# Query projection of a cross-attention kernel: seven block products of one Strassen level in place of eight

## What is computed

```python
# latents: 8 batches x 112 rows, 1024 wide; Wq: 1024 x 4096 (32 heads of 128)
q = (latents @ Wq).reshape(b, q_len, N_KV_HEADS, N_GROUPS, HEAD_DIM)
k = (hidden_states @ Wk).reshape(b, kv_len, N_KV_HEADS, HEAD_DIM)
v = (hidden_states @ Wv).reshape(b, kv_len, N_KV_HEADS, HEAD_DIM)
scores = jnp.einsum('bqhgd,bkhd->bhgqk', q, k) * scale
attn = jax.nn.softmax(scores.astype(jnp.float32), axis=-1).astype(q.dtype)
out = jnp.einsum('bhgqk,bkhd->bqhgd', attn, v)
```

## Time and profile before

| | us |
|---|---|
| median of 3 runs | 1857.2 |
| the runs | 1855.57, 1857.20, 1857.59 |
| the profiled execution | 1857.21 |
| its span, first to last instruction | 1855.3 |
| PE busy in the span | 1824.4 (98%) |
| ACT, DVE, POOL busy | 599.2, 636.9, 588.8 |

### The profile page before, as it was taken

How to read it: one execution, slowest core, us unless ns; L and a number is a source line. 1 busy time by engine, 2 the same in 40 slices (tenths; PEclk the granted TensorE clock), 3 DMA queues, 4 the chain that set the end, 5 groups by cost and what they waited for, 6 DMA issues and landing times.

```text
span 1855.3 us, 26708 instructions
## 1 busy us (share of the span) xinstructions
PE 1824.4 (98%) x9446; PEld 1645.2 (89%) x9446; DVE 636.9 (34%) x1114; ACT 599.2 (32%) x1156; POOL 588.8 (32%) x392
## 2 busy tenths in 40 slices
PE   8999999999999999999999999999999999999996
PEld 7989989799999988989998999899888988998886
DVE  3611122111111137713761475157344422212216
ACT  3221212122222246713761475157422213202321
POOL 2121200022222236533452255235455322222242
PEclk9999999999999999999999999999999999999998
DMA  8444412343654534422441244134244221111134
GB/s 276 156 163 153 148 68 108 93 140 124 207 187 134 176 127 156 142 79 68 151 151 61 86 162 127 51 113 139 100 144 163 80 97 51 57 57 53 49 102 170
DMA packets 108974, 225.78 MB, mean 122 GB/s; under 512 B 14976, under 2 KB 73344, under 8 KB 108032
## 3 DMA queue, kind: packets, MB, share of 16 engines
q1 hardware_dynamic: 108928, 225.14, 36.1%
...
## 4 chain that ended last, share of the span: by engine, by line
PE 68%; issue 21%; POOL 8%; DVE 1%; ACT 1%; DMA 0%; POOLq 0%; SPq 0%; ACTq 0%; DVEq 0%
PE bank L1133 22%; PE bank L1134 22%; PE bank L1135 22%; POOL tile_region L608 6%; POOL slab_split L577 2%; PE bank L1294 1%; PE bank L1166 0%; ACT slab_split L649 0%; PE bank L1195 0%; DVE small L863 0%; DMA mid_region<-k_latents_scratch 0%; DVE mid_region L856 0%; DMA slab_raw<-in_wkv 0%; POOLq L607 0%; DVE tile_region L1109 0%
## 5 line engine op out<-in xcount | busy, mean ns | idle before, releaser
L577 POOL TENSOR_TENSOR slab_split<-slab_raw,slab_split 128x1024 fp32r<-128x1024 f32 x126 | 301.9, 2397 | 783.8 <-ACT slab_split L649 783.8
L1133 PE MATMUL bank<-act_region,slab_split 128*128 128x448 f32 (+2 forms) x1376 | 501.0, 364 | 1.7 <-DVE mid_region L856 1.3
L1135 PE MATMUL bank<-act_region,slab_split 128*128 128x448 f32 (+2 forms) x1376 | 501.0, 364 | 0.0
L1134 PE MATMUL bank<-act_region,slab_split 128*128 128x448 f32 (+2 forms) x1376 | 500.7, 364 | 0.0
L608 POOL TENSOR_TENSOR tile_region<-tile_region,small 128x487 f32<-128x487 f32 x224 | 215.9, 1001 | 219.7 <-DVE small L939 219.7
L1133 PEld LDWEIGHTS bank<-act_region,slab_split 128*128 128x128 f32 x1376 | 258.4, 188 | 28.9 <-issue 2.3
L1134 PEld LDWEIGHTS bank<-act_region,slab_split 128*128 128x128 f32 x1376 | 258.4, 188 | 25.6
L1135 PEld LDWEIGHTS bank<-act_region,slab_split 128*128 128x128 f32 x1376 | 258.3, 188 | 24.8
L649 ACT ACTIVATE slab_split<-slab_raw 128x1024 fp32r<-128x1024 f32 x126 | 133.0, 1057 | 389.4 <-PE bank L1135 378.6
L1133 PE MATMUL bank<-mid_region 128*128 128x488 f32 (+2 forms) x480 | 199.0, 415 | 3.0 <-DMA mid_region<-k_latents_scratch 2.5
L976 DVE TENSOR_TENSOR y_region<-y_region,bank 128x512 f32 (+2 forms) x96 | 59.5, 620 | 365.7 <-PE bank L1135 365.7
...
## 6 DMA issues: line engine op xcount, KB each, us to landing
slab_raw<-in_slabs SPq DMA_DIRECT2D x126, 512.0 KB, 3.5
q_scratch<-y_region SPq DMA_DIRECT2D x16, 1792.0 KB, 7.6
...
```

The costliest lines, as they stand in the source:

```text
L577: pool.tensor_tensor(WS[s][1], RAWS[s], f32(WS[s][0]), ALU.subtract).then_inc(s_wlo, 1)
L1133: pe.matmul(out_ap, w[0], a[0], start=first, stop=False)
L1134: pe.matmul(out_ap, w[0], a[1], start=False, stop=False)
L1135: return pe.matmul(out_ap, w[1], a[0], start=False, stop=last)
```

## The change

A pair of heads is now one block product. The weights of the pair are a 2x2 of blocks (two heads, two halves of the contraction), the latents another (two halves of the contraction, two halves of the rows). Plain multiplication takes 8 block products of 4 k each; one level of Strassen's scheme (in Winograd's form) takes 7, of sums of blocks, and adds the results up.

- Four sums of latent blocks' halves (T1 to T4) are made once: nine steps and four splits on DVE (`row_sums`), four hi parts on ACT, 1792 columns each, between the `kl` and `vl` units. The `vl` units now take batches 4 to 7 first.
- For each pair POOL makes four sums of weight blocks from the two raw slabs, then the lo parts of seven blocks; ACT makes the seven hi parts (`block_hi`). Each block is 128x512. The seven split blocks WB and the raw slabs have one buffer each.
- For each pair PE runs seven products of 4 k x 3 = 12 matmuls of 448 columns. ACT copies the first product to SBUF; DVE makes seven sums (`combine`) that end in four half results C22, P1C, C21 and C12, in this order; ACT and DVE split these into QST.
- SP loads both slabs of a pair together and stores the pair's queries as before. The score tiles of the first step stand behind products 4, 5 and 6 of the last pair. Loads of the first two attention steps move, and the buffers of queries, keys and values in RB lie elsewhere.

```diff
+BLOCKS = ("A11", "S2", "S3", "S1", "A12", "A22", "S4")
+N_Q = len(BLOCKS)
+N_COMB = 7
+LAST_QUAD = {3: (0, 1, 2), 4: (3, 4), 5: (5, 6)}
...
         RAWS = [part(RAW, s * SLAB, SLAB) for s in range(2)]
...
+        def x_block(h, kh):
+            return [XT[h][:, l, 4 * kh:4 * kh + 4, :] for l in range(2)]
+
+        B11, B21, B12, B22 = x_block(0, 0), x_block(0, 1), x_block(1, 0), x_block(1, 1)
+        T2, T3, T4 = [t_block(RB, i * 2 * T_WORDS) for i in range(3)]
+        T1 = B12
+        TRAW = [part(YR, i * T_WORDS, T_WORDS).rearrange("p (k n) -> p k n", k=4) for i in range(2)]
...
+        WB = [[part(RC, (2 * i + l) * 512, 512) for l in range(2)] for i in range(4)]
+        WB += [[part(RD, (2 * i + l) * 512, 512) for l in range(2)] for i in range(2)]
+        WB += [[part(RA, l * XT_AT + 2 * NK * HALF, 512) for l in range(2)]]
+        SRAW = [part(FB, i * 512, 512) for i in range(4)]
+        WSRC = [RAWS[0][:, 0:512], SRAW[1], SRAW[2], SRAW[0], RAWS[0][:, 512:1024], RAWS[1][:, 512:1024], SRAW[3]]
+        W21 = RAWS[1][:, 0:512]
+        P1C, U3, C22, C21 = [part(FB, at, HALF) for at in (2048, 2496, 2944, 3500)]
+        U2, C12 = [part(YR, 8 * ROWS + i * HALF, HALF) for i in range(2)]
...
+            def load_pair(j):
+                for s in range(2):
+                    sp.dma_start(RAWS[s], slabs[T_Q + 2 * j + s]).then_inc(s_rawq, 16)
+
+            load_pair(0)
...
+                    if n == N_UNITS - 1:
+                        sp.wait_ge(s_blo, N_Q - 1)
+                        load_pair(1)
...
-            def store_pair(kv, g, c, slot):
-                sp.wait_ge(s_ev, c + 1)
+            def store_pair(j):
+                kv, g, slot = j // 4, 2 * (j % 4), j % 2
+                sp.wait_ge(s_qlo, FREE + 4 * (j + 1))
                 sp.dma_start(q_d[kv, :, :, :, g * SQ:(g + 2) * SQ].rearrange("p b l c -> p (b l) c"),
                              part(YR, slot * 4 * ROWS, 4 * ROWS).rearrange("p (b c) -> p b c", b=2 * B)
                              ).then_inc(s_qst[slot], 16)
...
-            q_heads(0)
...
-            with sp.Fori(2, NKV) as kv:
-                q_heads(kv)
+            store_pair(0)
+            for j in range(1, PAIRS):
+                if j < PAIRS - 1:
+                    sp.wait_ge(s_blo, N_Q * j + N_Q - 1)
+                    load_pair(j + 1)
+                else:
+                    sp.wait_ge(s_blo, N_Q * PAIRS)
+                    for s in range(2):
+                        sp.dma_start(RAWS[s], slabs[T_WO + s]).then_inc(s_raw[s], 16)
+                    sp.wait_ge(s_q, N_Q * j + 3)
+                    load_qk(0, 1, 1, 1)
+                    load_v(0, 1, 1, 1)
+                store_pair(j)
+                if j == 8:
...
+                    load_qk(0, 0, 0, 0)
+                if j == 10:
+                    load_v(0, 0, 0, 0)
...
             for s in range(2):
                 sp.wait_ge(s_qst[s], FREE + 16 * PAIRS // 2)
...
-            slab_lo(0, 0)
-            slab_lo(1, 1)
-            pool.wait_ge(s_mm, C_Q)
...
-            slabs_lo(2, NH - 2, 0)
+            def weight_blocks_lo(j):
+
+
+                for n, (out, a, b, op) in enumerate([(SRAW[0], W21, WSRC[5], ALU.add), (SRAW[1], SRAW[0], WSRC[0], ALU.subtract),
+                                                     (SRAW[2], WSRC[0], W21, ALU.subtract),
+                                                     (SRAW[3], WSRC[4], SRAW[1], ALU.subtract)]):
+                    if n == 0:
+                        pool.wait_ge(s_rawq, 32 * (j + 1))
+                    elif n != 2:
+                        pool.wait_ge(s_sum, 4 * j + (n + 1) // 2)
+                    pool.tensor_tensor(out, a, b, op).then_inc(s_sum, 1)
+                for n in range(N_Q):
+                    pool.wait_ge(s_bhi, N_Q * j + n + 1)
+                    pool.tensor_tensor(WB[n][1], WSRC[n], f32(WB[n][0]), ALU.subtract).then_inc(s_blo, 1)
+
+            pool.wait_ge(s_clo, B - 1)
+            weight_blocks_lo(0)
...
+            with pool.Fori(1, PAIRS) as j:
+                pool.wait_ge(s_blo, N_Q * j)
+                weight_blocks_lo(j)
...
+            def block_hi(j, n):
+
+                if BLOCKS[n][0] == "S":
+                    act.wait_ge(s_sum, 4 * (j + 1))
+                else:
+                    act.wait_ge(s_rawq, 32 * (j + 1))
+                act.activation(WB[n][0], WSRC[n], ACT.Copy).then_inc(s_bhi, 1)
...
+            def q_quad(j, r, i, last=False):
+
+                def next_hi(n):
+
+                    act.wait_ge(s_q, N_Q * j + n + 1)
+                    if not last:
+                        block_hi(j + 1, n)
...
+                def queries_hi(n, gg, h, src):
+                    act.activation(q_half(r, 0, gg, h), batches(src), ACT.Copy, scale=SCALE).then_inc(s_qhi, 1)
+
+                act.wait_ge(s_q, N_Q * j + 1)
+                act.wait_ge(s_qlo, FREE + 4 * j - 2)
+                act.activation(P1C, GB[0][:, 0:HALF], ACT.Copy).then_inc(s_p1, 1)
+                for n in range(3):
+                    next_hi(n)
+                act.wait_ge(s_qst[r], FREE + 16 * i)
+                act.wait_ge(s_comb, FREE + N_COMB * j + 3)
+                queries_hi(j, 1, 1, C22)
+                next_hi(3)
+                act.wait_ge(s_comb, FREE + N_COMB * j + 5)
+                queries_hi(j, 0, 0, P1C)
+                next_hi(4)
+                act.wait_ge(s_comb, FREE + N_COMB * j + 6)
+                queries_hi(j, 1, 0, C21)
+                next_hi(5)
+                act.wait_ge(s_comb, FREE + N_COMB * j + 7)
+                queries_hi(j, 0, 1, C12)
+                next_hi(6)
...
+            def q_quad(j, r, last=False):
+
+                def combine(n, product, out, a, b, op):
+
+                    dve.wait_ge(s_comb, FREE + N_COMB * j + n)
+                    dve.wait_ge(s_q, N_Q * j + product)
+                    dve.tensor_tensor(out, a, b[:, 0:HALF], op).then_inc(s_comb, 1)
...
+                dve.wait_ge(s_p1, j + 1)
+                dve.wait_ge(s_qlo, FREE + 4 * j)
+                combine(0, 2, U2, P1C, GB[1], ALU.add)
+                combine(1, 3, U3, U2, GB[2], ALU.add)
+                combine(2, 4, C22, U3, GB[3], ALU.add)
+                combine(3, 4, U2, U2, GB[3], ALU.add)
+                queries_lo(0, 1, 1, C22)
+                scores(3)
+                combine(4, 5, P1C, P1C, GB[0], ALU.add)
+                queries_lo(1, 0, 0, P1C)
+                scores(4)
+                combine(5, 6, C21, U3, GB[1], ALU.subtract)
+                queries_lo(2, 1, 0, C21)
+                scores(5)
+                combine(6, 7, C12, U2, GB[2], ALU.add)
+                queries_lo(3, 0, 1, C12)
...
+            def step(i, dst, a, b, op):
+
+                if i:
+                    dve.wait_ge(s_tr, i)
+                dve.tensor_tensor(dst, a, b, op).then_inc(s_tr, 1)
+
...
+            def row_sums(u):
+
+                R0, R1 = TRAW
+                if u == 4:
+                    dve.wait_ge(s_lnlo, 2 * B)
+                    step(0, R0, f32(B22[0]), f32(B12[0]), ALU.subtract)
+                if u == 5:
+                    step(1, R0, R0, f32(B22[1]), ALU.add)
...
+                if u == 12:
+                    row_sum_lo(2, T1, R1)
+                if u == 15:
+                    row_sum_lo(3, T4, R0)
...
-            with pe.Fori(0, NH // 2 - 2) as i:
-                for s in range(2):
-                    pe.wait_ge(s_wlo, 2 * i + s + 1)
-                    for h in range(2):
-                        product(s, of_xt, h, 0, NK, 0, C_Q + 4 * i + 2 * s + h, C_Q + 2 * s + h)
+            def q_quad(j, between, rows_ready=True):
+
+                def query_product(n, t, dst):
+
+                    pe.wait_ge(s_blo, N_Q * j + n + 1)
+                    for k in range(4):
+                        last = three(dst[:, 0:HALF], [WB[n][l][:, k * P:(k + 1) * P] for l in range(2)],
+                                     [t[l][:, k, :] for l in range(2)], k == 0, k == 3)
+                    last.then_inc(s_q, 1)
+
+                pe.wait_ge(s_comb, FREE + N_COMB * j - 2)
+                query_product(0, B11, GB[0])
...
+                pe.wait_ge(s_comb, FREE + N_COMB * j - 1)
+                query_product(1, T2, GB[1])
+                pe.wait_ge(s_comb, FREE + N_COMB * j)
+                query_product(2, T3, GB[2])
...
+                query_product(3, T1, GB[3])
+                between(3)
+                pe.wait_ge(s_p1, j + 1)
+                query_product(4, B21, GB[0])
+                between(4)
+                if not rows_ready:
+                    pe.wait_ge(s_tlo, 4)
+                pe.wait_ge(s_comb, FREE + N_COMB * j + 1)
+                query_product(5, T4, GB[1])
+                between(5)
+                pe.wait_ge(s_comb, FREE + N_COMB * j + 2)
+                query_product(6, B22, GB[2])
...
+            q_quad(PAIRS - 1, first_scores)
+            pe.wait_ge(s_pad, 7)
+            pe.wait_ge(s_comb, FREE + N_COMB * PAIRS)
```

247 lines of the change are left out of this document (150 added, 97 removed).

## The result

| | before | after |
|---|---|---|
| median, us | 1857.24 (1855.57 to 1857.59) | 1932.85 (1929.66 to 1934.2) |
| span of the profiled execution, us | 1855.3 | 1930.1 |
| granted clock, mean of the span | 0.996 | 0.973 |
| query stage, first matmul to first transpose, us | 316.6 | 391.3 |

The change makes the kernel slower: ratio 1.0406, 95% interval 1.0388 to 1.0424. Forecast were 1911 us and 1884 to 1930; the time lies 2.9 us above that range and 21.9 above the forecast.

The account below looks back on a forecast made before the run. A ring of waits through the slabs, not PE, bounds the query stage: 7.9 + 10.1 + 5.2 = 23.2 us a pair. The stage reaches 370.4 us against 316.6, +53.8, giving 1911 us, range 1884 to 1930.

Parts of the forecast that it names:

- What can be gained: PE in the query stage: 84 matmuls a pair in place of 96, 38.9 us over 16 pairs at most.
- Duration of a POOL operation on 512 columns: POOL's weight sums and lo parts: 1.25 us each, 1.05 to 1.44; four sums with waits 5.2 us.
- From the store to both slabs landed: SP's slab load queued behind the query store: 10.1 us from store start to both slabs landed, 8.9 to 10.5.
- The rival in which the slabs come early enough: Query stage: store to slabs landed takes below 4 us, PE never waits, kernel 1821 us; chance 9%.
- The start and the ends: Query stage: pair 0's store at 19.1 us, pair 2's sums at 34.4; attention loads delay slabs 3.8 and 1.3 us.
- From the sums to the store: ACT's and DVE's alternating splits and combines, from POOL's four weight sums to SP's store: 7.9 us a period.
- POOL's sixth lower part, the load's other condition: POOL, which the load of pair j+2 also waits for: ready about 7.5 us after the sums, before the store.
- The low clock: PE after each idle stretch: half clock for 3 us, losing 1.5 us, hidden within each period.
- the ring: Query stage: weight sums, splits, store, slab load and sums again, 23.2 us a pair against PE's 17.03.
- The rival in which it stays low: PE's clock stays low over 12 us of each pair: 2096 us, or partly 1930 to 2000; chance 8%.
- Row sums: DVE's latent sums beside PE's units cost nothing; rival: uncovered, up to 28 us more, 1939 us, chance 3%.
- The signs: Profile: PE idle 4 to 6 us a pair, pairs 23 us apart, long ACT and POOL waits, store and load back to back.

Follow-up runs that it names:

- Kernel f: Changed kernel with the three raw-slab blocks first among the products and the load of pair j+2 ahead of the store of pair j: 1821.08 us.
- a: Changed kernel with SP issuing the load of pair j+2 ahead of the store of pair j, all else the same: 1858.54 us.
- kernel e: Changed kernel with POOL subtracting only 16 of 512 columns in each lower part from the second pair on, output wrong: 1910.06 us.
- g: Kernel f with the store of pair j put ahead of the load of pair j+2 again on SP's queue: 1906.88 us.
- c: Changed kernel with C22 summed in place in PSUM, so DVE's first query split has one SBUF operand: 1924.42 us.
- d: Changed kernel with ACT's hi part of each weight sum waiting for its own sum, not all four: 1928.21 us.

## Why the prediction was right in kind and too low by 22 us

- **What can be gained.** 84 matmuls a pair, 38.9 us at most: right. Kernel f is 37.4 us faster than the kernel before.
- **Duration of a POOL operation on 512 columns.** Taken 1.25 us out of 1.05 to 1.44; the rows have 1.26 to 1.30. Right, when DVE does not stand beside it. Four sums were given 5.2 us and took 5.1.
- **From the store to both slabs landed.** Taken 10.1 us; measured 10.3. Right. The rival in which the slabs come early enough fell with it.
- **The start and the ends.** Store of pair 0 at 19.1 us into the stage, measured 384.95 - 365.81 = 19.1. Last sum of pair 2 ready at 34.4, measured 34.7. The loads of attention behind pairs 8 and 10 were given 3.8 and 1.3 us more; two of the distances between sums are 28.57 and 26.10 us, 3.8 and 1.3 above the 24.8 of the others. All right.
- **From the sums to the store: the term that failed.** Taken 7.9 us, measured 9.4. I took DVE's split at 0.62 us from the earlier trace rows, where one operand lies in PSUM (`y_region<-bank,y_region`). The split of the changed kernel has both operands in SBUF, and two of four lie beside a running POOL: 1.25 and 1.68 us. That is 0.63 + 1.06 = 1.7 us a period, 1.6 net in the period of 24.8 against 23.2. 13 periods and the first chain, 14 x 1.6, are 22.4 us. The time was 21.9 over the forecast. Its price could have been read before. Line 1066 of the kernel before has two SBUF operands on DVE, and of its four executions on 512 columns one starts beside a running POOL. DVE's timeline, then POOL's:

```profile
1474.90 0.69 DVE L1066 TENSOR_TENSOR act_region<-tile_region,act_region 128x512 fp32r<-128x512 f32 x1 [0.70 <-ACT act_region L813]
...
1479.77 1.05 DVE L1066 TENSOR_TENSOR act_region<-tile_region,act_region 128x512 fp32r<-128x512 f32 x1 [0.70 <-ACT act_region L813]
```
```profile
1477.87 2.40 POOL L577 TENSOR_TENSOR slab_split<-slab_raw,slab_split 128x1024 fp32r<-128x1024 f32 x1 [8.07 <-ACT slab_split L649]
```

  POOL's instruction ends at 1480.27, and DVE's, started inside it, 0.55 us behind that, at 1480.82; alone it takes 0.69. The right price of a split beside POOL was thus a range, 0.62 to 0.62 plus most of one POOL instruction of 1.25. Four splits at 1.1 us more would have put the upper end of the period at 27.6 and that of the time near 1970. The spread that I gave (21.3 to 24.2 for the period) had no share for the splits at all, and 24.8 lies outside it. Its sum is also slightly off: 1911 less 25 and plus 14 are 1886 and 1925, not 1889 and 1926.
- **POOL's sixth lower part, the load's other condition.** Taken 7.5 us behind the sums; it ends at 409.29, 8.8 behind them, since it waits 0.6 us for ACT and two of POOL's instructions (402.88 and 405.73) come second to DVE's splits. It is not the last wait here, as forecast, but by 0.6 us only, and with the store out of the way (a) it sets the period.
- **The low clock.** Forecast was 3 us at half rate behind each wait, hidden by the ring. Behind the first wait it is so: PE's matmuls take 0.57 us in place of 0.37 from 404.7 to 407.7, and the granted clock is 0.57 in 404 to 407 and 1.00 in 411 to 415. But only behind the first two of the 14 waits is the clock low for 3.5 to 3.8 us; behind the twelve others it is low for 7.0 to 7.3 us, in part while PE still waits (0.50 in 453 to 459 and in 681 to 687, for instance). In each period 7 to 16 matmuls fall into it and lose 1.3 to 2.8 us. That costs no time, since PE still waits 5.6 us on average in each period. The clock came back each time, and in kernel e it does so within a ring of the size that was forecast. The rival in which it stays low fell.
- **Row sums.** Covered: PE's first product starts 0.4 us later than before and no wait on them stands among the large ones. That rival fell too.
- **The signs.** PE idle 5.6 us on average once a pair for DVE, POOL's and ACT's long waits for the slabs, ACT's 4.6 us for the sums, store and load back to back: all as named. Pairs are 24.8 us apart and not 23.

Causes shown by an edit of their own: the load behind the store (a, g), the exclusion (c, e, and against my expectation d and g), and that the saving is there once the ring is open (f). In f two edits are together; g and a take them apart. Read from rows and not shown by an edit of its own: that the 20.1 us in a are the ring through POOL's sixth lower part. Of the 74.3 us that a gains, 70.8 are found in the stage; the rest isn't followed.
